# A two-layer CIN with a small tower on one core: the direct half of layer 1 is summed in one chain per tile that ends in PSUM, and layer 0's last 32 rows are multiplied in fp32

## What is computed

```
e = stack of 32 gathered rows                    # [512, 32 fields, 32 d]
def cin(x0, prev, W):                            # W: [fields * len(prev), 128]
    z = einsum('bhd,bmd->bhmd', x0, prev).reshape(b, h * m, d)
    return relu(einsum('bpd,pn->bnd', z, W))
c0 = cin(e, e, filter_0);  c1 = cin(e, c0, filter_1)
z = concat([sum_d c0, sum_d c1, dense_ctx])      # [512, 128 + 128 + 16]
y = relu(relu(z @ W_top1 + b_top1) @ W_top2 + b_top2) @ W_top3
```

## Time and profile before

| what | us |
|---|---|
| median of 3 runs | 1007.62 (1007.05 to 1007.86) |
| profiled execution, device time | 1010.25 |
| its span in the trace | 1008.4 |
| PE busy in the span | 889.1 (88%) |
| DVE busy | 879.3 (87%) |
| POOL busy | 687.8 (68%) |
| ACT busy | 646.0 (64%) |
| mean granted TensorE clock | 0.985 |

### The profile page before, as it was taken

The page is one execution under the profiler, slowest core; times in us unless marked ns, Lnnn a source line. Parts: engine busy times, 40 slices in busy tenths (PEclk is TensorE's granted clock), DMA queues, the critical chain, the costliest instruction groups (busy, mean ns, idle before and its releaser), DMA issues.

```text
span 1008.4 us, 13290 instructions
## 1 busy us (share of the span) xinstructions
PE 889.1 (88%) x3444; PEld 643.1 (64%) x3444; DVE 879.3 (87%) x2377; ACT 646.0 (64%) x2174; POOL 687.8 (68%) x436
## 2 busy tenths in 40 slices
PE   0349999999999999997999999997999999999977
PEld 0126777676767766765766777675767767766743
DVE  1124889999999999996999999997999999999992
ACT  2118777777776777665677776765776767767711
POOL 6758787665666888885666888885665665656630
PEclk9989999999999999998999999998999999999998
DMA  9052222212111222212011222211111112210000
GB/s 249 12 172 85 72 70 71 69 58 93 61 48 46 71 73 72 72 62 82 32 66 69 73 71 73 72 62 45 68 69 69 69 68 69 69 54 5 2 1 0
DMA packets 34671, 66.66 MB, mean 66 GB/s; under 512 B 6225, under 2 KB 19761, under 8 KB 30402
## 3 DMA queue, kind: packets, MB, share of 16 engines
q1 hardware_dynamic: 27570, 59.94, 17.5%
q0 software_dynamic: 4096, 2.11, 1.6%
q10 hardware_dynamic: 2928, 3.76, 1.2%
HBM read 62.64 MB, written 5.24 MB: 67 GB/s over the span
## 4 chain that ended last, share of the span: by engine, by line
PE 41%; DVE 25%; issue 20%; POOL 7%; ACT 5%; DMA 1%; DVEq 0%; POOLq 0%; ACTq 0%
DVE acc L509 20%; PE acc L605 7%; PE yd L587 6%; PE ya L587 5%; PE ya L589 5%; PE yd L588 5%; PE ya L588 5%; PE yd L589 5%; POOL emb L256 4%; ACT scaled L405 3%; DVE fold_b L523 2%; POOL half L275 1%; DVE sum L496 1%; ACT small_split L391 1%; POOL part L279 1%
## 5 line engine op out<-in xcount | busy, mean ns | idle before, releaser
L405 ACT ACTIVATE scaled<-ya,emb 128x128 f32<-128x128 f32 x2048 | 583.6, 371 | 253.1 <-PE ya L589 250.9
L275 POOL TENSOR_TENSOR half<-scaled 128x1024 f32<-128x1024 f32 x128 | 308.1, 2407 | 229.2 <-ACT scaled L405 228.7
L509 DVE SCALAR_TENSOR_TENSOR acc<-yd,emb,acc 128x128 f32<-128x128 f32 x1536 | 415.7, 342 | 8.3 <-PE yd L589 8.2
L587 PE MATMUL yd<-w_hi,prev_hi 128*128 128x512 f32 x512 | 246.8, 482 | 38.0 <-issue 27.4
L279 POOL TENSOR_TENSOR part<-half 128x512 f32<-128x512 f32 x128 | 196.1, 1532 | 17.8
L587 PE MATMUL ya<-w_hi,prev_hi 128*128 128x512 f32 x512 | 203.2, 397 | 4.7 <-issue 2.5
L588 PE MATMUL yd<-w_lo,prev_hi 128*128 128x512 f32 x512 | 201.9, 394 | 0.0
L589 PE MATMUL yd<-w_hi,prev_lo 128*128 128x512 f32 x512 | 201.6, 394 | 0.0
L589 PE MATMUL ya<-w_hi,prev_lo 128*128 128x512 f32 x512 | 201.1, 393 | 0.0
L588 PE MATMUL ya<-w_lo,prev_hi 128*128 128x512 f32 x512 | 200.9, 392 | 0.0
L587 PEld LDWEIGHTS yd<-w_hi,prev_hi 128*128 128x128 f32 x512 | 96.6, 189 | 116.6 <-DVE acc L509 57.1
(11 more groups left out here) (53 smaller groups left out, 399.2 us busy)
## 6 DMA issues: line engine op xcount, KB each, us to landing
xb<-xt_scratch SPq DMA_DIRECT2D x32, 1024.0 KB
x<-xt_scratch SPq DMA_DIRECT2D x64, 192.0 KB
xm<-xt_scratch SPq DMA_DIRECT2D x32, 256.0 KB
emb<-in_tbl,idx POOLq DMA_INDIRECT x128
scaled<-in_L_rec_filter SPq DMA_DIRECT2D x8, 256.0 KB
xt_scratch<-xt_stage SPq DMA_DIRECT2D x7, 256.0 KB
xt_scratch<-xt_stage SPq DMA_DIRECT2D x9, 128.0 KB
w_second_index_twice<-in_L_rec_filter ACTq DMA_DIRECT2D x2, 512.0 KB
```

What stands on the lines that cost most here:

```text
L275: pool.tensor_tensor(half[:], piece[:, 0:AB * C // 2], piece[:, AB * C // 2:AB * C], ALU.add).then_inc(halved, 1)
L405: op = act.activation(scaled[:, tile % PR, C * j + N * i:C * j + N * (i + 1)], ya[:, n % RA, N * i:N * (i + 1)], ACT.Copy, scale=scale_of( ...
L509: op = dve.scalar_tensor_tensor(acc[:, c % 2, q, i, :], yd[:, n % RD, N * i:N * (i + 1)], scale_of(c, q, HB * j + i), before, ALU.mult, AL ...
L587: pe.matmul(dst, v_hi, m_hi, start=start, stop=False)
```

## The change

Four things change together.

1. **One chain per tile.** `add_banks` takes the banks of both tiles of a pair in one slot and goes field by field, tile 0 and tile 1 in turns. All 16 fields of a tile are added into one accumulator `acc[:, t, :]` of 128 columns, which starts from `part[.., 0, :]`. Each STT waits for the one two places ahead of it (`chained`, one step per STT). It starts when both banks are there. The last STT of a tile writes back into its `yd` bank.
2. **No folds over the chunk.** `finish_pair` runs in slots 3 and 7: three tensor_tensor on 2 x 128 columns add the other three pieces of `part` to that total in PSUM, each waiting for the one ahead of it, and one STT on 256 columns applies the relu and adds to `sum1`. `finish_a`, `finish_b` and `finish_c` are gone. `sum1` has a place per block, and one tensor_tensor of DVE on 512 columns at the very end takes the place of POOL's `fold1`.
3. **The bank rotation.** PE's banks for field group 1 of a pair wait until `finish_pair` of the pair before has ended (`summed1`), since the total lies in that bank; the other groups wait for the last STT on the bank (`chained`).
4. **Layer 0's 32 rows.** `x16` is loaded once, the product `small` stays fp32 (two buffers), and `layer0_rest` is an fp32 matmul with K = 32 on unsplit weights. `small_high`, `small_low` and the split of the weights are gone.

Beside these, `emb` holds all four blocks, 20 gathers of block 1 instead of 16 are issued before the loop, and the other 76 are spread evenly over the tiles of the first 20 chunks, with no wait.

```diff
-    emb = sb("emb", [P, 2, F * D])
+    emb = sb("emb", [P, BT, F * D])
+    EARLY_NEXT = 20
+    GATHER_CHUNKS = 20
...
+            def add_banks(c, pair, j):
+                g = 2 * c + pair
+                n = d_number(c, 2 * pair, j)
+                dve.wait_ge(d_ready, n + 2)
                 if j == 0:
+                    dve.wait_ge(part_ready, DC * c + 2 * pair + 2)
+                for i in range(HB):
+                    for t in range(2):
+                        q, slot = 2 * pair + t, (n + t) % RD
+                        y_part = yd[:, slot, N * i:N * (i + 1)]
+                        before = part[:, c % 2, q, 0, :] if i == j == 0 else acc[:, t, :]
+                        after = y_part if (j, i) == (DB - 1, HB - 1) else acc[:, t, :]
+                        if (i, j) != (0, 0):
+                            dve.wait_ge(chained, chain_count(g, j, i, t) - 2)
+                        elif g > 0:
+                            dve.wait_ge(chained, PAIR_STEPS * g)
+                        dve.scalar_tensor_tensor(after, y_part, scale_of(c, q, HB * j + i), before,
+                                                 ALU.mult, ALU.add).then_inc(chained, 1)
+
+            def finish_pair(c, pair):
+                g, bt = 2 * c + pair, c // CPB
+                slot = d_number(c, 2 * pair, DB - 1) % RD
+                total = yd[:, slot:slot + 2, N * (HB - 1):N * HB]
+                for k in range(1, HB):
+                    dve.wait_ge(chained, PAIR_STEPS * (g + 1) - HB + k)
+                    dve.tensor_tensor(total, total, part[:, c % 2, 2 * pair:2 * pair + 2, k, :], ALU.add).then_inc(chained, 1)
...
             def bank_d(c, q, j):
                 n, fields = d_number(c, q, j), slice(HB * j, HB * (j + 1))
-                if n >= RD:
-                    pe.wait_ge(d_used, n - RD + 1)
+                g, t = 2 * c + q // 2, q % 2
+                if j >= 2:
+                    pe.wait_ge(chained, chain_count(g, j - 2, HB - 1, t))
+                elif g > 0 and j == 0:
+                    pe.wait_ge(chained, chain_count(g - 1, DB - 2, HB - 1, t))
+                elif g > 0:
+                    pe.wait_ge(summed1, g)
...
             def layer0_rest(c):
-                pe.wait_ge(small_lo_ready, c + 1)
-                pe.matmul(acc0[:], w16_split[:], small_split[:], start=False, stop=True).then_inc(l0_done, 1)
+                pe.wait_ge(small_ready, c + 1)
+                pe.matmul(acc0[:], w16[:], small[:, c % 2, :], start=False, stop=True).then_inc(l0_done, 1)
...
             for c in range(CHUNKS + 1):
                 for s in range(SLOTS):
...
                     if c > 0:
-                        add_bank(c - 1, 2 * pair + 1, j)
-                    if s == 5 and c > 1:
-                        finish_a(c - 2)
...
+                        add_banks(c - 1, s // 4, s % 4)
+                    if c + 1 < CHUNKS and s < KT:
+                        product(c + 1, s)
+                    if c > 0 and s % 4 == 3:
+                        finish_pair(c - 1, s // 4)
```

More of the change, by code:

```diff
@@ L74, in cin_tower @@
         xm = sb("xm", [P, C])
-        x16 = sb("x16", [3 * F, 2, C])
+        x16 = sb("x16", [F, 2, C])
         whole = sb("whole", [P, 2, C])
-        small = sb("small", [3 * F, C])
-        small_split = sb("small_split", [3 * F, C], F32R)
+        small = sb("small", [F, 2, C])
         prev_hi = sb("prev_hi", [P, 3, C], F32R)
@@ L115, in cin_tower @@
         h2 = xb[:, 0:H2 // P, :]
-        y = small[0:1, :]
+        y = small[0:1, 0, :]
         ids_loaded = sem("ids_loaded")
@@ L265, in _ @@
             pool.wait_ge(later_ids_loaded, 16)
-            for f in range(16):
+            for f in range(EARLY_NEXT):
                 gather(1, f, gathered[1])
@@ L295, in small_product @@
             def small_product(c):
                 pool.wait_ge(x16_loaded, 32 * (c + 1))
[L297 to L308, removed]
+                if c > 1:
+                    pool.wait_ge(l0_done, c - 1)
@@ L310, in _ @@
+                pool.tensor_tensor(small[:, c % 2, :], x16[:, 0, :], x16[:, 1, :], ALU.mult).then_inc(small_ready, 1)
+            later = [(bt, f) for bt in range(1, BT) for f in range(F)][EARLY_NEXT:]
+            per_tile = [len(later) * k // (DC * GATHER_CHUNKS) for k in range(DC * GATHER_CHUNKS + 1)]
             small_product(0)
             for c in range(CHUNKS):
-                some = gathers_of(c)
+                if c + 1 < CHUNKS:
+                    small_product(c + 1)
                 for q in range(DC):
@@ L314, in _ @@
                     sum_tile(c, q)
[L315 to L320, removed]
+                    if c < GATHER_CHUNKS:
+                        for bt, f in later[per_tile[DC * c + q]:per_tile[DC * c + q + 1]]:
+                            gather(bt, f, gathered[bt])
@@ L385, in copy_xm @@
                 act.activation(xm_ps[:], xm[:], ACT.Copy).then_inc(xm_in_psum, 1)
[L387 to L391, removed]
             def prev_high(c):
@@ L525, in finish_c @@
-            def finish_c(c):
-                bt = c // CPB
-                dve.wait_ge(fin_b, c + 1)
-                if c % CPB == 0:
-                    if bt > 0:
-                        dve.wait_ge(folded1, 2 * bt - 1)
-                    dve.tensor_scalar(sum1[:], fold_b[:], 0.0, None, ALU.max).then_inc(summed1, 1)
-                else:
-                    dve.wait_ge(summed1, c)
-                    dve.scalar_tensor_tensor(sum1[:], fold_b[:], 0.0, sum1[:], ALU.max, ALU.add).then_inc(summed1, 1)
+                    dve.wait_ge(part_ready, DC * c + 2 * pair + 2)
@@ L536, in _ @@
             for k in range(KT):
                 product(0, k)
-            small_low(0)
             prev_low(0)
```

121 lines of the change are left out of this document (31 added, 90 removed).

## The result

The changed kernel takes 1018.98 us (median of 4 runs, 1017.65 to 1019.11) against 1007.74 us: 1.0109 times the time of before, 95% interval 1.0091 to 1.0126. It is slower by 11 us, where 1003.5 was forecast and 1016.0 was the upper end of the range.

The account below looks back on a forecast made before the run. PE and DVE were both nearly full, with DVE setting the pace. Turning chunks -10.9, chunks 0 and 1 +0.7, start +4.7, end +1.4 and regular chunks 0.0 sum to -4.1 us: 1003.5 forecast, range 991 to 1016.

Parts of the forecast that it names:

- The mechanism of the regular chunk: Regular chunks: PE's work of 26.34 us plus 1.41 for a finish_pair wait gives 27.75 against 27.74, no gain.
- The new rest is of layer0's form with fewer rows, and I take the same 0.90: PE, once a chunk: the fp32 K = 32 matmul was priced at 0.90 us, where the old rest cost 0.20.
- The dependent step: DVE's finish_pair: an operation on 2 x 128 columns with its total in PSUM, 0.41 us plus 0.04, 0.45 a step.
- the estimate of 0.39: DVE's finish_pair: a step's duration by the Trainium skill page's PSUM-to-SBUF figure, 0.39 us, the sum about 2 us lower.
- The first rival: PE's wait for finish_pair: dearer dependent steps, 0.50 instead of 0.41 us, give +10.4 us, 1013.9; chance 0.20.
- The chain's waits undo the overlap: DVE's STTs: each waiting STT starts only after the one ahead ends, +75 us, 1078; chance 0.07.
- The gathers: Three turning chunks: gathers arrive in time, so the sort no longer waits; 89.4 us against 100.3, -10.9.
- the rival by which they stay late: Chunks 14 and 22: gathers share POOL's queue with its sums and these chunks stay at 35 us, +11, 1014; chance 0.05.
- The start: Before the loop: four more gathers +5.1, small_high and small_low gone -1.4, three more passes +1.0; sum +4.7 us.
- Chunks 0 and 1: First chunks: chunk 1 +0.7 for the matmul and +0.6 for a shorter wait, chunk 0 -0.6; together +0.7 us.
- The end: Chunk 31 and after: waits of both pairs 1.4 and 0.9, cheaper folding -0.3, POOL's detour -0.6; sum +1.4 us.
- The profiled execution: Whole kernel: -4.1 us on the profiled 1010.25 gives 1006.1; with runs 2.6 lower, 1003.5 was predicted.

Follow-up runs that it names:

- e2: Changed kernel with the old split fp32r K = 96 treatment of layer 0's 32 rows put back; 988.58 us, 0.9807 of before.
- e5: Changed kernel with DVE's addition to sum0 moved behind finish_pair of slot 7; 1001.93 us, 0.9943 of before.
- e6: Changed kernel with POOL folding each tile's four pieces to two, so finish_pair has one dependent tensor_tensor instead of three; 986.77 us, 0.9789 of before.
- e1: Changed kernel with layer 0's 32 rows padded by zeros to a K-tile of 128 rows; 1007.0 us, 0.9988 of before.
- e7: Changed kernel with layer 0's 32 rows padded by zeros to 64 rows; 1020.52 us.
- e9: Changed kernel with layer 0's 32 rows padded by zeros to 96 rows, fp32; 1006.99 us.
- e3: Kernel before with emb for four blocks, no wait for it and evenly spread gathers, 16 of block 1 ahead of the loop; 993.89 us, 0.9854 of before.
- e4: Changed kernel with 16 gathers of block 1 ahead of the loop instead of 20; 1011.95 us, 1.0043 of before.
- e8: Changed kernel with the old fp32r rest, sum0 behind finish_pair, two pieces from POOL and 16 gathers ahead of the loop; 934.94 us, 0.9275 of before.

## Why the prediction was wrong, point by point

- **The mechanism of the regular chunk was right, its two prices were not.** "The chunk lasts 26.34 + 1.41 = 27.75": DVE's relief bought nothing, PE was paced by its own work plus one wait per chunk at slot 1 for the end of `finish_pair` (e2 shortens the work, e5 and e6 the wait, and the chunk follows each). It was 28.16, 0.41 more. The 26 regular chunks, forecast at no change, became 10.0 us longer, of 15.5 us missed.
- **The step that failed** is "The new rest is of layer0's form with fewer rows, and I take the same 0.90". It took 1.21 (0.31 of the 0.41). With fewer rows it is not of the same form: with 32 rows, and with 64, the load of its weights and that of the tile behind it do not run under the matmul ahead, which costs 0.39 us that 96 and 128 rows do not pay (e1, e7, e9). The price stood in the text without a lower or upper bound, though no row showed a narrow tile between full ones. With the tile padded to full height (e1) the chunk is 27.80 and the time 1007.0, and of the 3.5 us that are left to the forecast, 2.7 are the offset below: the rest of the reckoning nearly holds.
- **The dependent step** was taken at 0.45 and is 0.467, its duration 0.431 instead of 0.41; the wait cost 1.53 instead of 1.41. The steps make some 0.06 of that 0.12, the other half is spread over the stretch ahead of them (slot 6's STTs start 2.37 us into the slot and not 2.25). That the estimates met it so closely is partly luck, since the step's price came by a slope from other operations; the estimate of 0.39 named beside it was too low as well. Writing PSUM is not the cause to any large degree: an STT on 128 columns into PSUM takes 0.349, into SBUF 0.341 (means of the groups by form), and the step that reads PSUM and writes SBUF takes 0.424.
- **The first rival**, dearer finishing steps, had the right sign and place (PE's wait), and e6 bears out what it gives a step (0.46 a chunk for each). But at the measured 0.467 from step to step it makes only 2 us; the dearer part was on PE.
- **The chain's waits undo the overlap**: they do not; the STTs start 0.258 apart as before.
- **The gathers**: -10.1 in the turning chunks against -10.9 forecast; e3 shows them alone, and the rival by which they stay late is out.
- **The start**: +4.35 against +4.7. **Chunks 0 and 1**: +2.4 against +0.7. Chunk 1 grew by 2.0 instead of 1.3. The rest makes 1.0 of it (e2 has 26.35 there, against 27.36); the other 1.0 is not the wait that the prediction counted, since e5 and e6 leave chunk 1 at 27.4, and stays open. Chunk 0 did not get shorter (20.48 against 20.10); the other kernels with the new chain have 18.9 to 20.5 there, and why it differs stays open. **The end**: +2.0 against +1.4.
- **The profiled execution** of before lay 2.6 us above its median, that of the changed kernel (1018.88) did not. Carrying the offset over cost 2.7 of the 15.5 us.
- **The signs** that it named came in the main: the wait of 1.27 us (1.3), DVE idle for 4.4 us a chunk (3 to 4), the steps 0.467 apart (0.45), the turning chunks at 30.1 (29.8), the first prev_low at 75.32 (75.7), but the regular chunk of 28.16 lies outside its 27.6 to 27.9.

By parts, the change is: gathers -14 (e3 against before); chain and finish_pair with the old rest, measured with the four early gathers, -5 (e2 against e3); the fp32 rest on top, with K = 32, +30 (1018.98 - 988.58), of which 12 are the narrow tile (e1). The four gathers ahead of the loop are 7 in e4, of which their own time is 5.

## What to carry to other kernels

When two engines are equally full, taking work from one is only worth what the other has left: cost the new period on the second engine first, with every wait that its buffers now have. Taking a small job off an engine with slack by making it longer on the engine without is a loss, here 1 us a chunk. A matmul of 32 or 64 rows between full ones broke the overlap of weight loads; padding with zeros to 96 or 128 rows restored it (heights between 64 and 96 were not run). A chain that ends in a buffer that another engine waits for should have as few dependent steps behind it as can be, and what is not urgent belongs behind them.

## What the runs showed of the hardware that was not expected

- In a stream of full tiles, an fp32 matmul of 512 columns cost PE 0.39 us more with 32 or 64 rows than with 96 or 128: 0.09 lie ahead of it (0.95 against 0.86 from the start of the one before) and 0.30 behind it.
- The STTs, each with a wait on the one two places ahead, start as close together (0.258 us at 0.34 each) as they did without.
- A 32-row subtraction on DVE with two SBUF operands (small_low) took 1.66 us in the kernel before, beside POOL's sum into `part` (413.32 to 414.60), and 0.68 us in e2 at 414.67, where POOL had no sum under way (only the end of a gather, to 414.92). In e8 it took 1.44 us from 419.23, beside POOL's sum of 418.83 to 420.12. Both long ones end 0.54 to 0.55 us after POOL's sum, as if they had waited for it.
